# Expert products in split float32r: gate and up weights and rows in two parts, three passes each

## What is computed

```python
def _moe(x_flat, Wr, Wg, Wu, Wd):
    T = x_flat.shape[0]
    logits = x_flat @ Wr.T
    top_logits, top_idx = jax.lax.top_k(logits, TOP_K)        # 2 of 8
    probs = jax.nn.softmax(top_logits, axis=-1)
    cw = jnp.zeros((T, NUM_EXPERTS), x_flat.dtype)
    cw = cw.at[jnp.arange(T)[:, None], top_idx].add(probs)
    hg = jnp.einsum('eih,th->eti', Wg, x_flat)                # 256 -> 512, gate
    hu = jnp.einsum('eih,th->eti', Wu, x_flat)                # 256 -> 512, up
    y = jnp.einsum('ehi,eti->eth', Wd, jax.nn.silu(hg) * hu)  # 512 -> 256, down
    return jnp.einsum('eth,te->th', y, cw)
...
    return residual + moe_out
```

## Time and profile before

| | us |
|---|---|
| median of 3 runs (768.36 to 769.21) | 769.14 |
| the profiled execution's own time | 771.2 |
| its span, first to last instruction | 769.4 |
| TensorE busy | 603.2 (78%) |
| VectorE busy | 478.2 (62%) |
| ScalarE busy | 276.4 (36%) |
| GpSimd busy | 263.1 (34%) |

### The profile page before, as it was taken

The page is one execution under the profiler, slowest core; times in us unless marked ns, Lnnn a source line. Parts: engine busy times, 40 slices in busy tenths (PEclk is TensorE's granted clock), DMA queues, the critical chain, the costliest instruction groups (busy, mean ns, idle before and its releaser), DMA issues.

```text
span 769.4 us, 10430 instructions
## 1 busy us (share of the span) xinstructions
PE 603.2 (78%) x3606; PEld 402.4 (52%) x3606; DVE 478.2 (62%) x1048; ACT 276.4 (36%) x535; POOL 263.1 (34%) x242
## 2 busy tenths in 40 slices
PE   3933667877576869999549998888878799999990
PEld 2721445655452658888215555455445556666660
DVE  6869997969767865594577877867764211221223
ACT  1376433323101222354206664554535332222220
POOL 3157557645275643456661001001025001111111
PEclk9975769989867999999558999999989999999996
DMA  5101200000011300259996664260003958888835
GB/s 184 53 27 55 78 2 0 1 1 0 0 45 36 83 0 1 77 104 167 205 234 83 84 83 58 31 84 1 3 22 119 331 216 289 306 293 280 302 143 177
DMA packets 45779, 81.93 MB, mean 106 GB/s; under 512 B 7424, under 2 KB 37312, under 8 KB 42784
## 3 DMA queue, kind: packets, MB, share of 16 engines
q1 hardware_dynamic: 43856, 76.15, 38.5%
q0 software_dynamic: 1872, 5.13, 1.7%
HBM read 65.56 MB, written 15.51 MB: 105 GB/s over the span
## 4 chain that ended last, share of the span: by engine, by line
PE 38%; DVE 10%; DMA 3%; issue 2%; ACT 2%; POOL 1%; SPq 0%; POOLq 0%; DVEq 0%; ACTq 0%
PE bank L745 19%; DVE small L1671 5%; PE bank L992 4%; PE bank L969 4%; PE bank L942 4%; PE bank L739 4%; DMA pieces<-P 2%; PE bank L944 1%; PE bank L971 1%; POOL P L2071 1%; DVE mtok L1682 1%; PE bank L1009 1%; DMA yt<-results 1%; ACT PTa L1257 1%; DVE XA L1700 0%
## 5 line engine op out<-in xcount | busy, mean ns | idle before, releaser
L1671 DVE TENSOR_REDUCE small<-bank 128x1 f32<-128x256 f32 (+3 forms) x256 | 107.5, 482 | 14.1 <-PE bank L944 13.2
L745 PE MATMUL bank<-wb,xt 128*128 128x512 f32 x184 | 82.8, 592 | 0.0
L1976 POOL TENSOR_TENSOR al<-hm,ah 128x512 fp32r<-128x512 f32 (+1 forms) x28 | 40.9, 1462 | 92.0 <-ACT ah L1220 92.0
L942 PE MATMUL bank<-Ks,Qs 96*128 96x256 bf16 (+3 forms) x256 | 67.5, 331 | 5.3 <-DVE small L1671 3.7
L1915 DVE TENSOR_TENSOR bhm<-bsg,bank 128x512 f32<-128x512 f32 x23 | 15.8, 688 | 83.8 <-PE bank L745 83.8
L969 PE MATMUL bank<-Qs,Ks 99*128 99x512 bf16 (+3 forms) x256 | 59.5, 309 | 7.2 <-issue 6.8
L944 PE MATMUL bank<-maskb,identb 128*128 128x128 bf16 x256 | 55.8, 236 | 0.0
L1542 DVE TENSOR_TENSOR_SCAN S<-AT,U 128x512 f32<-128x512 f32 x32 | 49.7, 1553 | 8.2 <-POOL QS L1994 7.9
L1257 ACT ACTIVATE PTa<-bank 128x512 f32<-128x512 f32 (+1 forms) x96 | 43.7, 528 | 30.4 <-PE bank L971 30.1
L1257 ACT ACTIVATE PTb<-bank 128x512 f32<-128x512 f32 (+1 forms) x96 | 43.7, 529 | 28.4 <-PE bank L971 28.0
L969 PEld LDWEIGHTS bank<-Qs,Ks 99*128 99x128 bf16 x256 | 25.5, 100 | 49.3 <-issue 32.4
(11 more groups left out here) (332 smaller groups left out, 1517.0 us busy)
## 6 DMA issues: line engine op xcount, KB each, us to landing
wb<-e_pack SPq DMA_DIRECT2D x23, 1536.0 KB, 7.0
pieces<-P SPq DMA_DIRECT2D x12, 512.0 KB, 10.0
Qs<-pieces SPq DMA_DIRECT2D x48, 128.0 KB, 5.4
Ks<-pieces SPq DMA_DIRECT2D x48, 128.0 KB, 6.1
stg<-w_pack SPq DMA_DIRECT2D x18, 256.0 KB, 2.7
wf<-t_pack SPq DMA_DIRECT2D x12, 256.0 KB, 2.7
sorted_rows<-blank SPq DMA_DIRECT2D x1, 2944.0 KB, 13.5
yt<-results SPq DMA_DIRECT2D x8, 256.0 KB, 5.0
```

The costliest lines, as they stand in the source:

```text
L745: last = nc.tensor.matmul(outap, a, b_, start=start and i == 0, stop=stop and i == n - 1, **kw)
L942: nc.tensor.matmul(banks[b][:, o:o + w], Q[0:96, h, i * P:(i + 1) * P], K[0:96, h, 0:w], start=True, stop=False)
L1671: last = nc.vector.tensor_reduce(mxv[:, i, h:h + 1], banks[b][:, o:o + w], AX.X, ALU.max, negate=True)
L1976: nc.gpsimd.tensor_tensor(al[0:M, s % 3, :], hm[0:M, s % 3, :], ah[0:M, s % 3, :].bitcast(F32), ALU.subtract).then_inc(*alr.tick(s))
```

## The change

The gate and up weights of each block are split into `wh` (float32r) by ScalarE and `wl`, the rest, by VectorE, a half (gate or up, 128x1024) at a time; the turned rows likewise into `xh` and `xl` in place of `xt`. Both are held twice. Gate and up are then three single-pass products for each of the two chunks, 12 in all a block, in place of four plain float32 ones. The down product stays as it was, on the raw weights in `wb`.

The step `bw` (block, half) is new in ORDER: the first half of block i+1 stands ahead of `gu` of block i, the second behind it and ahead of `dn` of block i-1 and `ht` of block i. TensorE no longer waits for the weights' DMA but for `wl`; ScalarE and VectorE now do. For block 0, ScalarE waits for the last score products, since `wh` and `wl` take memory of the stacks of the heads.

Tiles move: `rows` now holds blocks 0 to 7, `xga` blocks 8 to 18 in the memory of XTh and XTl, and is loaded behind the last output projection; `wb2` takes the place of the old `xga`, so its load waits only for the last split of packed weights, and `wb3` waits for the last attention sums.

```diff
-XG_PARTS = [(0, XGA), (XGA, XGA + NC * CH // P), (XGA + NC * CH // P, BLOCKS)]
+XG_PARTS = [(0, NC * CH // P), (NC * CH // P, NC * CH // P + XGA), (NC * CH // P + XGA, BLOCKS)]
...
-        ORDER.append(("bx", 0))
+        ORDER += [("bx", 0), ("bw", 0, 0), ("bw", 0, 1)]
         for i in range(BLOCKS):
             if i + 1 < BLOCKS:
-                ORDER.append(("bx", i + 1))
+                ORDER += [("bx", i + 1), ("bw", i + 1, 0)]
             ORDER.append(("gu", i))
+            if i + 1 < BLOCKS:
+                ORDER.append(("bw", i + 1, 1))
             if i >= 1:
                 ORDER.append(("dn", i - 1))
             ORDER.append(("ht", i))
...
                 elif i == 2:
+                    sp.wait_ge(*w_split.upto(len(JOBS) - 1))
+                elif i == 3:
                     sp.wait_ge(*pv.upto(QUADS - 1))
...
             for i in range(2):
                 block_weights(i)
-            sp.wait_ge(*w_split.upto(len(JOBS) - 1))
             for j in range(2):
                 sp.wait_ge(s_put[j], 16 * NT)
             sorted_part(0)
-            sorted_part(1)
             for i in range(2, NWB):
                 block_weights(i)
             sp.wait_ge(*mm.upto(("wout", 3, 1)))
+            sorted_part(1)
             sorted_part(2)
...
             def block_in(i):
 
-                xt = moe["xt"][:, i % 2]
-                pe.wait_ge(*bxh.upto(i))
-                pe.wait_ge(s_wb[i % NWB], 16 * (i // NWB + 1))
+                xh, xl = moe["xh"][:, i % 2], moe["xl"][:, i % 2]
+                pe.wait_ge(*bxl.upto(i))
                 for half, who in ((0, bgate), (1, bhid)):
                     b = 2 * half + i % 2
                     claim(b, who, i)
-                    w = raw_half(i, half)
-                    product(banks[b][:], [(xt[:, k], w[:, k]) for k in range(KC)]).then_inc(*mm.tick(("gu", i, half)))
+                    pe.wait_ge(*wsl.upto((i, half)))
+                    wh, wl = moe["wh"][:, i % 2, half], moe["wl"][:, i % 2, half]
+                    terms = []
+                    for k in range(KC):
+                        terms += [(xh[:, k], wh[:, k]), (xl[:, k], wh[:, k]), (xh[:, k], wl[:, k])]
+                    product(banks[b][:], terms).then_inc(*mm.tick(("gu", i, half)))
...
+                elif op == "bw":
+
+                    _, i, half = it
+                    act.wait_ge(s_wb[i % NWB], 16 * (i // NWB + 1))
+                    if i == 0:
+                        act.wait_ge(*mm.upto(("st", N_HEADS - 1, 2)))
+                    elif i >= 2:
+                        act.wait_ge(*mm.upto(("gu", i - 2, half)))
+                    nc.scalar.copy(moe["wh"][:, i % 2, half], raw_half(i, half)).then_inc(*wsh.tick((i, half)))
...
+                elif op == "bx":
+
+                    i = it[1]
+                    dve.wait_ge(*bxh.upto(i))
+                    if i >= 2:
+                        dve.wait_ge(*mm.upto(("gu", i - 2, 1)))
+                    nc.vector.tensor_tensor(moe["xl"][:, i % 2], banks[6][:, 0:D].rearrange("p (k n) -> p k n", k=KC),
+                                            moe["xh"][:, i % 2].bitcast(F32), ALU.subtract).then_inc(*bxl.tick(i))
+                elif op == "bw":
+
+                    _, i, half = it
+                    dve.wait_ge(*wsh.upto((i, half)))
+                    dve.wait_ge(s_wb[i % NWB], 16 * (i // NWB + 1))
+                    nc.vector.tensor_tensor(moe["wl"][:, i % 2, half], raw_half(i, half), moe["wh"][:, i % 2, half].bitcast(F32),
+                                            ALU.subtract).then_inc(*wsl.tick((i, half)))
```

More of the change, by code:

```diff
@@ L149, in build @@
         XA = sb("XA", [NT, D], F32)
+        xt_at = cursor[0]
         XTh = sb("XTh", [KC, NC * CH], F32R)
@@ L224, in build @@
         assert o <= slot_at[0] + 32768
-        m, _ = plan([("wb2", [EW], F32)], slot_at[1])
+        m, o = plan([("wb2", [EW], F32)], x1_at + 10240)
+        assert o <= mlp_at
         moe.update(m)
-        m, o = plan([("xga", [XGA, ROW], F32)], x1_at + 10240)
-        assert o <= mlp_at
+        m, _ = plan([("wh", [2, 2, KC, EI], F32R), ("wl", [2, 2, KC, EI], F32R)], slot_at[1])
+        moe.update(m)
+        m, o = plan([("xga", [XGA, ROW], F32)], xt_at)
+        assert o <= x1_at
         moe.update(m)
@@ L234, in block_rows_of @@
         def block_rows_of(i):
-            if i < XGA:
-                return moe["xga"][:, i, :]
+            if i < NT:
+                return rows[:, i, :]
             if i < XGA + NT:
-                return rows[:, i - XGA, :]
+                return moe["xga"][:, i - NT, :]
             return moe["xgc"][:, i - XGA - NT, :]
@@ L243, in build @@
         moe.update(m)
-        m, o = plan([("bsg", [2, EI], F32), ("bhm", [2, EI], F32), ("hT", [2, EI], F32), ("xt", [2, KC, P], F32)], mlp_at)
+        m, o = plan([("bsg", [2, EI], F32), ("bhm", [2, EI], F32), ("hT", [2, EI], F32), ("xh", [2, KC, P], F32R),
+                      ("xl", [2, KC, P], F32R)], mlp_at)
         assert o <= mlp_at + 20480
@@ L343, in build @@
         share_set = tally("row_shares_set")
-        bxh = tally("block_rows_turned")
+        wsh = tally("block_weights_high")
+        wsl = tally("block_weights_low")
+        bxh = tally("block_rows_high")
+        bxl = tally("block_rows_low")
         bgate = tally("block_gate")
@@ L695, in sorted_part @@
                 src = sorted_rows[b0 * P:b1 * P, :].rearrange("(b p) d -> p b d", p=P)
-                dst = (moe["xga"][:], rows[:], moe["xgc"][:])[j]
+                dst = (rows[:], moe["xga"][:], moe["xgc"][:])[j]
                 sp.dma_start(dst, src).then_inc(s_xg[j], 16)
@@ L1006, in block_transposes @@
                 pe.wait_ge(s_xg[rows_part(i)], 16)
-                claim(6, bxh, i)
+                claim(6, bxl, i)
                 for k in range(KC):
@@ L1357, in _ @@
                         act.wait_ge(*mm.upto(("gu", i - 2, 1)))
-                    nc.scalar.copy(moe["xt"][:, i % 2], banks[6][:, 0:D].rearrange("p (k n) -> p k n", k=KC)).then_inc(*bxh.tick(i))
+                    nc.scalar.copy(moe["xh"][:, i % 2], banks[6][:, 0:D].rearrange("p (k n) -> p k n", k=KC)).then_inc(*bxh.tick(i))
+                elif op == "bw":
[6 more added lines that the diff above has]
+                    nc.scalar.copy(moe["wh"][:, i % 2, half], raw_half(i, half)).then_inc(*wsh.tick((i, half)))
                 elif op == "gu":
```

## The result

The changed kernel took 782.15 us, the median of four runs (777.68 to 786.60), against 769.17 before (768.36 to 769.50): a ratio of 1.017 with a 95% interval of 1.011 to 1.023. It is 13 us slower. The profiled execution, 786.6 us with a span of 784.5, is the longest of the four, so what its profile shows is some 4 us more than the median has.

The account below looks back on a forecast made before the run. The prediction took a two-block loop through load, casts, subtracts and scaling, 6.35 us a block against 5.82 before, as the bound. With a 1.5 us later start, the last scaled result came 10.2 later: 769.14 to 779.3 us, range 766 to 789.

Parts of the forecast that it names:

- the loop over two blocks: Expert blocks: scaled result, buffer freed, load, cast, subtracts, gate-times-up, next scaling; 12.70 us for two blocks, 6.35 a block.
- The landing, taken at 7.0: Time from a weight load's issue to its arrival inside the loop, taken as the median of 7.0 us.
- the likeliest case: Block stage bound by the two-block loop with landings of 6.7 to 7.3: 775 to 785 us, chance 0.68.
- coefficient of ten: The landing counts ten times, once in the start and nine in the loop: 0.1 us is worth 1 us.
- The first rival: Weight loads land sooner: 776.3 us at 6.7, 764.3 at 5.5; chance 0.10 of being faster than before.
- The rest of the loop, taken at 5.70: Everything in the 12.70 us loop but the landing: issue, hand-overs, cast, two subtracts, gate-times-up, scaling and gaps.
- 5.16 a block: TensorE's need in each block with single passes: products, transposes and down together 5.16 us, against 5.82 before.
- The 1.5 us later start: Start of the block stage: block 0's turn ends at 622.85 in place of 621.3, 1.5 us later.
- a granted clock under 1.00: Sign of being wrong: TensorE's granted clock falling below 1.00 in the block stage.
- the fourth rival: TensorE, idle 1.2 us in each 6.35, loses its clock lastingly: some 80 us more, 860; chance 0.04.
- the slack of 2 us: Room in the block stage in which single clock dips of a few us on TensorE disappear, save in the start.
- The second rival: The loop in the block stage doesn't bind and TensorE does: 756 us, or about 765 with a three-block loop; chance 0.06.

Follow-up runs that it names:

- e3: The changed kernel with five weight buffers in place of four, engine order kept: 756.3 us, ratio 0.986.
- e5: The changed kernel with each block's load cut in two, gate and up reloaded once the block four back is split, down as before: 755.4 us, ratio 0.982.
- e10: The changed kernel with loads from block 4 on cut to gate and up (1 MB), stale down weights used: 768.9 us, ratio 0.989.
- e6: The changed kernel run once more, unaltered, for a second profile: 786.4 us.
- e2: The changed kernel with gate and up again plain float32 products of the raw weights; casts, subtracts and waits kept: 780.5 us, ratio 1.020.
- e7: The kernel of e2 run once more for a second profile: 779.5 us in a single run.
- e1: The changed kernel with the result of block i-1 scaled ahead of the second subtract of block i+1: 777.3 us, ratio 1.012.
- e9: The changed kernel with both casts of block i+1 behind the silu of block i, and gate-times-up and scaling each one subtract earlier: 782.5 us, ratio 1.006.
- e4: The kernel before with one more plain float32 product of 128x512 a block ahead of the up products: 788.8 us, one run.
- e8: The kernel before with four more float32r single passes of 128x512 a block on TensorE: 792.6 us, one run.
- e11: The kernel before with the whole up product made twice in each block: 819.3 us, one run, beside 778.1 for the kernel before.
- e12: The kernel before with the changed kernel's casts and subtracts made beside it into a scratch tile: 776.8 us, one run, beside 778.1.

## Why the prediction was right, point by point

**The bound and the loop.** That TensorE's 5.82 us a turn would be replaced by the loop over two blocks, through VectorE's order and the buffer's release, was right, and was shown from three sides: by the chain after, by opening the loop (e3, e5) and by shortening its landing (e10). The sizes fit too. From one landing to the next issue the profile after has 5.20 us (653.03 + 9.44 = 662.47 to 667.67), so a turn should be (5.20 + landing) / 2. The means of the nineteen later landings and of the spacings of the loads:

| kernel | mean landing | (5.20 + landing) / 2 | measured spacing |
|---|---|---|---|
| changed | 8.45 | 6.83 | 6.77 |
| changed, second profile (e6) | 8.09 | 6.64 | 6.67 |
| plain products (e2) | 6.99 | 6.10 | 6.10 |
| plain products, second profile (e7) | 7.36 | 6.28 | 6.30 |

The fit of the plain products is closer than it should be, since TensorE is on their chain for a part. Where the loop was shortened TensorE takes over sooner: e1, with 5.20 less the 1.14 of a subtract, gives 6.14 and measured 6.26.

**The landing, taken at 7.0, was too small.** It is the term that was mis-sized most: "issue to landing 7.0" in the sum of the loop, and 8.45 and 8.09 in the mean of the two profiles. I asked only whether a landing could get shorter and made 7.3 the upper end of the likeliest case, from the rows of one kernel in which nothing depended on a late load. At the coefficient of ten that the prediction gave, 1.1 to 1.45 us are 11 to 14 us. The first rival, loads that land sooner, had the sign wrong: at a DMA share of 0.70 in place of 0.82 no landing was under 6.9 in the changed kernel. The Trainium skill (DMA: Bandwidth & Descriptors, Latency and other measured facts) says that lighter HBM load makes the fixed cost of a DMA smaller. The traces of this case don't show it: before, at the higher share, the shortest was 6.7.

**The rest of the loop, taken at 5.70, was 0.50 too large.** Cast 1.04 and subtract 1.22 were right. The hand-overs were not: the landing to the cast took 0.02, not 0.12, and VectorE begins an operation before the end of the one ahead of it, which I had with a gap of 0.04. I had read that gap from two additions (lines 1932 and 1933) of which the program makes the second wait for the first. Here are the operations of one turn, with the load that follows:

```profile
663.57 1.23 DVE L1953 TENSOR_TENSOR wl<-wb,wh 128x1024 fp32r<-128x1024 f32 x1 [3.46 <-ACT wh L1381]
664.71 0.68 DVE L1938 TENSOR_TENSOR bhm<-bsg,bank 128x512 f32<-128x512 f32 x1
665.31 1.22 DVE L1953 TENSOR_TENSOR wl<-wb,wh 128x1024 fp32r<-128x1024 f32 x1
666.45 0.47 DVE L1961 TENSOR_SCALAR ys<-bank,rows 128x256 f32<-128x256 f32 x1
667.67 0.34 SPq L702 DMA_DIRECT2D wb<-e_pack  x1
```

663.57 + 1.23 is 664.80, and the next starts at 664.71: three such steps take 0.37 off. Nine laps of 0.50 are 4.5 us, which hid a part of the landing's excess. From the 781.4 forecast for the profiled execution, less 4.5 and with 14.5 and 10.9 for the landings, come 791.4 and 787.8. Measured were 786.6, with a stage that began 2.6 us earlier than in the profile before (612.74 for 615.30), and 786.4. So the two terms account for the profiles within some 2 us. The median of the runs, 782.2, is 2.9 above the forecast of 779.3, and no run tells which landings its executions had. That it came so near is in part luck: the two errors had opposite signs, and the executions without a profile were shorter than the two with one.

**The products.** 0.233 us a single pass and 5.16 a block were right, as e3's spacing shows, and so was that TensorE's gain would not be seen: e2 without it took 780.5. (Half of the drain to each leaves 3.44 and 1.72, not 3.45 and 1.71; the sum is the same.)

**The start.** Gate-times-up of block 0 was put 6.3 us behind the first rows' transposes; it came 6.18 behind (612.74 to 618.92), before 4.82 (615.30 to 620.12). The 1.5 us later start was 1.4.

**The clock.** I named a granted clock under 1.00 as a sign of being wrong. It was 0.97 in the stage, so the fourth rival holds a small part. TensorE had stood still for 1.97 us until 665.45; the granted clock was 0.50 in 667 to 669, the products stepped at 0.43 us, and the chain ran through TensorE for that one lap (6.09 us of products from 666.32), where the slack of 2 us did not suffice. In the other laps it did, also in the second such stretch (0.50 in 735 to 738).

**The second rival**, that the order leaves slack and TensorE stays the bound, was given 0.06 and would be this kernel with one buffer more: its 756 is what e3 took (756.3).

## What to carry to other kernels

Before moving work behind a load onto another engine, write down what frees the buffer and follow it round: load, every step in front of the release on each in-order engine, release, load. The length of that loop divided by the number of blocks it spans is a bound like an engine's busy time, and neither the busy shares nor the sums by engine show it. When such a loop bound here, another buffer or an earlier release of the part that is no longer read was worth more than either reordering (e1, e9), and a loop that holds a DMA should be costed with landings longer than those of a kernel in which nobody waited for them.

## What the runs showed of the hardware that I had not expected

A load of 1.5 MB that lands in 7.0 us can take 9.8 (10.1 in e1), the last of it on one DMA engine alone in the load shown above (share 0.06), for stretches of several loads, and then return to 7.0. Landings of 8 us and more came in twelve and ten of nineteen loads in the two profiles of the changed kernel, in eleven of nineteen in e1 and eight of the fourteen known in e9. They came in none and three of nineteen with plain products, in none before and in e4, in two in e8 and one of fourteen in e11, and by its packets in at most one of nineteen in e12, which casts and subtracts the weights too. VectorE starts an operation up to 0.09 us before the one ahead of it ends.
